# Sums of squares over a head from a rounded part and its remainder, with the rounding on ScalarE and the subtraction on GpSimd

## The reference, cut to what matters

```python
def l2norm(t):
    return t / jnp.maximum(jnp.linalg.norm(t, axis=-1, keepdims=True), 1e-12)

def attn_layer(x, Wqkv, qs, ksc, Wo):        # 16 heads of 64, window 32
    qkv = x @ Wqkv
    q, k, v = jnp.split(qkv, 3, -1)
    ...
    q = l2norm(q) * qs
    k = l2norm(k) * ksc
    ...
    q = q * cos * scale + rotate_half(q) * sin * scale
    k = k * cos * inv + rotate_half(k) * sin * inv
    out = local_attention(q, k, v)
    return out @ Wo
```

## Time and profile before

| | |
|---|---|
| median of 3 runs | 4179.59 us (4172.83 to 4183.58) |
| the profiled execution | 4182.92 us, of which the span is 4181.1 us |
| PE busy | 3900.5 us, 93% of the span |
| DVE, ACT, POOL busy | 79%, 74%, 62% |
| stage 2 | about 700 us to 4090 us, six layers |

### The profile page before, as it was taken

One profiled execution on the slowest core, in us unless ns is written; L12 is line 12 of the kernel. 1 busy time (PEld: TensorE's weight loads), 2 busy tenths in 40 slices (PEclk: granted clock), 3 DMA queues, 4 the chain that ended last, 5 costly groups with the idle time before them and its releaser, 6 DMA issues.

```text
span 4181.1 us, 190344 instructions
## 1 busy us (share of the span) xinstructions
PE 3900.5 (93%) x78816; PEld 3039.7 (73%) x78816; DVE 3305.5 (79%) x5294; ACT 3091.6 (74%) x10376; POOL 2581.2 (62%) x2583
## 2 busy tenths in 40 slices
PE   6888885999998999989999989999899999899998
PEld 3555554888866888848888668888488887588884
DVE  6778874988866888938888668989489886698894
ACT  5877785888865888838888658888488886588883
POOL 4667765766645676627666456766377664566660
PEclk9999998999999999999999999999999999999999
DMA  1000001111111111111111111111111111111110
GB/s 35 2 2 2 2 2 53 47 45 45 46 56 38 45 47 45 44 50 44 49 44 46 58 36 47 44 49 42 53 44 47 47 44 61 35 45 46 47 43 26
DMA packets 100195, 167.40 MB, mean 40 GB/s; under 512 B 26224, under 2 KB 33648, under 8 KB 99056
## 3 DMA queue, kind: packets, MB, share of 16 engines
q1 hardware_dynamic: 99312, 154.89, 12.6%
HBM read 26.13 MB, written 2.10 MB: 7 GB/s over the span
## 4 chain that ended last, share of the span: by engine, by line
PE 69%; issue 9%; POOL 3%; DVE 1%; ACT 0%; DMA 0%; SPq 0%; POOLq 0%; DVEq 0%; ACTq 0%
PE s_bank L1177 13%; PE s_bank L1246 10%; PE s_bank L1259 9%; PE s_bank L1198 8%; PE s_bank L1157 5%; PE s_proj L1222 4%; PE s_proj L1223 4%; PE s_proj L1224 4%; PE s_bank L1209 2%; PE s_bank L1210 2%; PE s_bank L1211 2%; PE s_bank L1167 2%; PE s_bank L1140 1%; POOL s_rotated L802 1%; PE s_bank L1289 1%
## 5 line engine op out<-in xcount | busy, mean ns | idle before, releaser
L802 POOL TENSOR_TENSOR s_rotated<-s_rotated,s_by_sin 128x512 f32<-128x512 f32 x768 | 983.8, 1302 | 227.3 <-DVE s_by_sin L1087 225.2
L811 POOL TENSOR_TENSOR s_probs<-s_probs,s_rden 128x256 f32<-128x256 f32 x768 | 479.7, 641 | 729.8 <-DVE s_rden L1027 729.3
L901 ACT ACTIVATE s_probs<-s_bank,s_neg_max 128x64 f32<-128x64 f32 x3072 | 908.0, 310 | 5.7 <-DVE s_neg_max L1020 5.6
L783 DVE TENSOR_TENSOR s_qk<-s_rotated,s_inv_norm 128x1024 f32<-128x1024 f32 x384 | 743.8, 1937 | 11.5
L1082 DVE TENSOR_TENSOR s_rotated<-s_proj,s_cos 128x1024 f32<-128x1024 f32 x384 | 469.6, 1223 | 241.5 <-ACT s_sq L935 240.9
L901 ACT ACTIVATION_READ_ACCUMULATOR s_probs<-s_bank,s_neg_max 128x1 f32 x3072 | 636.1, 207 | 0.0
L891 ACT ACTIVATE s_probs_t<-s_bank 64x512 f32<-64x512 f32 x384 | 226.8, 591 | 524.8 <-PE s_bank L1157 524.8
L1177 PE MATMUL s_bank<-s_qk 32*32 32x64 f32 x49152 | 581.4, 223 | 26.3 <-issue 25.9
L1177 PEld LDWEIGHTS s_bank<-s_qk 32*32 32x32 f32 x49152 | 510.9, 103 | 115.4 <-issue 114.6
L213 POOL TENSOR_TENSOR s_probs<-s_probs,s_rden 128x384 f32<-128x384 f32 (+3 forms) x512 | 406.4, 802 | 206.1 <-DVE s_rden L406 202.2
L824 POOL TENSOR_TENSOR s_sq<-s_sq 128x512 f32<-128x512 f32 x384 | 490.2, 1277 | 65.5 <-ACT s_sq L935 59.8
(11 more groups left out here) (118 smaller groups left out, 8156.2 us busy)
## 6 DMA issues: line engine op xcount, KB each, us to landing
s_v<-s_v SPq DMA_DIRECT2D x384, 192.0 KB, 2.5
s_v<-s_v SPq DMA_DIRECT2D x384, 64.0 KB, 2.4
s_qk<-f_wqk SPq DMA_DIRECT2D x6, 1024.0 KB, 6.4
s_xs_raw<-u SPq DMA_DIRECT2D x48, 128.0 KB
s_xf<-u SPq DMA_DIRECT2D x48, 128.0 KB, 2.3
s_xs_raw<-u SPq DMA_DIRECT2D x48, 127.8 KB
s_xf<-u SPq DMA_DIRECT2D x48, 127.8 KB, 2.6
s_qk<-f_wv SPq DMA_DIRECT2D x6, 512.0 KB, 6.8
```

Of the source, the lines that this page charges most:

```text
L783: return nc.vector.tensor_tensor(qk[:, quad % 2, :, :, at:at + TOKS], rotated[:, par, :, :, :], by, ALU.mult)
L802: nc.gpsimd.tensor_tensor(rotated[:, par, :, half, :], rotated[:, par, :, half, :], by_sin[:, :, 1 - half, :], (ALU.subtract, ALU.add)[half])\
L811: nc.gpsimd.tensor_tensor(part, part, by, ALU.mult).then_inc(S["probs_done"], 1)
L901: last = nc.scalar.activation(probs[:, par, h, b, :], score_bank[h][:, b * KEYS:(b + 1) * KEYS], ACT.Exp, scale=-1.0, bias=neg_max[:, par, ...
```

## The change

The sum of the halves of `sq` is split into `sum_high`, the sum rounded to float32r, and `sum_rest`, the remainder. ScalarE rounds, GpSimd subtracts, and TensorE multiplies both parts with `same_head_r` (the same ones, cast to float32r once at the start by VectorE) in one-pass products that accumulate in `ss_bank`: four float32r products of 128x256 for two float32 ones. On TensorE they now stand behind the values (L1209 to L1211 of before), on ScalarE the rounding stands ahead of L891, on GpSimd the subtraction stands between L824 and L802. `sq` is still held until `ss_done`. The core of the diff:

```diff
+        same_head_r = sb("s2_same_head_r", [P, P], F32R)
...
+        sum_high = sb("s2_sum_high", [P, 2, TOKS], F32R)
+        sum_rest = sb("s2_sum_rest", [P, 2, TOKS], F32R)
...
                     nc.gpsimd.tensor_tensor(sq[:, :, 0, :], sq[:, :, 0, :], sq[:, :, 1, :], ALU.add)\
                       .then_inc(S["sqadd_done"], 1)
+                    pool.wait_ge(S["sum_high"], m + 1)
+                    nc.gpsimd.tensor_tensor(sum_rest[:, :, :], sq[:, :, 0, :], sum_high[:, :, :].bitcast(F32), ALU.subtract)\
+                      .then_inc(S["sum_rest"], 1)
                     pool.wait_ge(S["prod_done"], 2 * m + 2)
...
+                if live(s, p, LAG_MIX, first):
+                    m = n - LAG_MIX
+                    act.wait_ge(S["sqadd_done"], m + 1)
+                    if not (first and p == LAG_MIX):
+                        act.wait_ge(S["ss_done"], m)
+                    nc.scalar.activation(sum_high[:, :, :], sq[:, :, 0, :], ACT.Copy).then_inc(S["sum_high"], 1)
...
+            nc.vector.tensor_copy(same_head_r[:, :], same_head[:, :]).then_inc(S["cast"], 1)
...
-                if live(s, p, LAG_MIX, first):
-
-                    m = n - LAG_MIX
-                    pe.wait_ge(S["sqadd_done"], m + 1)
...
-                    for i in range(2):
-                        last = nc.tensor.matmul(ss_bank[:, i * TOKS:(i + 1) * TOKS], same_head[:, :],
-                                                sq[:, i, 0, :], start=True, stop=True)
-                    last.then_inc(S["ss_done"], 1)
...
+                if live(s, p, LAG_MIX, first):
+
+                    m = n - LAG_MIX
+                    pe.wait_ge(S["sum_rest"], m + 1)
...
+                    for i in range(2):
+                        nc.tensor.matmul(ss_bank[:, i * TOKS:(i + 1) * TOKS], same_head_r[:, :],
+                                         sum_high[:, i, :], start=True, stop=False)
+                        last = nc.tensor.matmul(ss_bank[:, i * TOKS:(i + 1) * TOKS], same_head_r[:, :],
+                                                sum_rest[:, i, :], start=False, stop=True)
+                    last.then_inc(S["ss_done"], 1)
```

More of the change, by code:

```diff
@@ L659, in build_stage2 @@
         hid = [[v_flat[:, c * SEQ:(c + 1) * SEQ] for c in range((par + 1) * NC, (par + 2) * NC)] for par in range(2)]
-        names = ("const_in consts cast zeroed attn_w ffn_w tables w_high w_rest xs_in xs_high xs_rest proj_done sq_done sqadd_done prod_done "
+        names = ("const_in consts cast zeroed attn_w ffn_w tables w_high w_rest xs_in xs_high xs_rest proj_done sq_done sqadd_done sum_high sum_rest prod_done "
                  "add_done ss_done guard_done log_done inv_done norm_done score_done max_done exp_done "
@@ L986, in _ @@
             dve.wait_ge(S["consts"], 4)
-            dve.wait_ge(S["cast"], 2)
+            dve.wait_ge(S["cast"], 3)
             def centre(f):
@@ L1125, in _ @@
             pe.wait_ge(S["consts"], 4)
-            pe.wait_ge(S["cast"], 2)
+            pe.wait_ge(S["cast"], 3)
             def ffn_mean(f):
@@ L1212, in step @@
                       .then_inc(S["v_mm"], 1)
+                if live(s, p, LAG_MIX, first):
+                    m = n - LAG_MIX
+                    pe.wait_ge(S["sum_rest"], m + 1)
+                    if not (first and p == LAG_MIX):
+                        pe.wait_ge(S["guard_done"], m)
+                    if full and not first and p == LN_STEP + 1:
+                        pe.wait_ge(S["f_xc"], l * NSEQ + s)
+                    if full and not first and p == LN_STEP + 2:
+                        pe.wait_ge(S["f_log"], l * NSEQ + s)
+                    for i in range(2):
[4 more added lines that the diff above has]
+                    last.then_inc(S["ss_done"], 1)
                 if full:
```

## The result

The changed kernel takes 4414.2 us in the median (4407.49 to 4415.18), the kernel before 4176.2 over the same rounds: a ratio of 1.0564, interval 1.0544 to 1.0584. The forecast of slower came true, at 238 us where 159 were forecast; 4414 lies within the range of 4215 to 4430. The profiled execution took 4413.94 us, 231 more than that of before.

A forecast was written before the change was run, and what follows sets the result against it. TensorE bounds the kernel before at 7.36 us a step; GpSimd was to take over at 6.93 + 0.98 = 7.91 us. A layer of 507.7 against 481.2 us gives +159 us over six layers, 4339 us; range 4215 to 4430.

The forecast's parts named there:

- the bound of 4426: Upper bound of the sum: hold 1.09, copy 0.70, subtraction 1.28 us make GpSimd's round 8.14 us, adding 87 us.
- The bound moves to GpSimd, at 7.91 us a step: GpSimd's round of 6.93 us plus a 0.98 us hold sets each step, in place of TensorE's 7.36 us.
- The exclusion between `write_qk` and GpSimd: VectorE's write_qk waits for the running GpSimd instruction, then holds the next for 0.98 us, now in each step.
- The handover: Between GpSimd's addition and subtraction: 0.09 us to ScalarE, its copy 0.61, 0.09 us back.
- The place of `write_qk`: Issued 2.6 us after GpSimd's addition starts, within the subtraction; over 1.5 us of margin on either side.
- the chance of 0.75: Chance given to the main forecast, resting on the exclusion's two readings and the margin around write_qk's place.
- TensorE's saving: TensorE's own work falls 0.40 us a step, 152 us in all, coming through only if TensorE stays the bound.
- the terms for the starts of a layer and for the special steps: Per layer: -3.4 us for three steps without normalising, +9.0 for seven token splits, +3.8 for seven layer-norm holds.
- Layer norm's division, +0.54 in step 7: Layer-norm division on VectorE holds GpSimd's normalising by 0.54 us seven times a layer, +3.8 us.
- The first: Rival: TensorE stays the bound and its 0.40 us a step come through, 4028 us; chance 0.07.
- the third: Rival: GpSimd's float32r subtraction costs more, say 1.65 us, 151 us more, 4490 us; chance 0.04.
- The second: Rival: write_qk finds a free place, GpSimd is not held, a two-step chain gives 7.26 us, 4142; chance 0.13 with mixtures.

The follow-up runs named there:

- experiment 4: Kernel before plus ScalarE's rounding and GpSimd's subtraction in their new places, both unused, TensorE's sums as before: 4328.6 us, 1.035 of the kernel before.
- experiment 1: Changed kernel with write_qk's second input from an idle PSUM bank, comparison for product, normalisation left out: 4220.3 us, 1.0099 of the kernel before.
- experiments 3: Kernel before plus one unused GpSimd subtraction of 128x512 between addition and rotations, without ScalarE: 4188.7 us, 1.0024 of the kernel before.
- experiment 6: Changed kernel with all its waits and places, but the two old float32 products instead of the four one-pass ones: 4463.5 us, 1.0691 of the kernel before.

## Why the prediction was right, and what was mis-sized

The mechanism came true as it was forecast. That 4414 lies inside the range, 16 us under its upper bound, is in part luck: the bound of 4426 came from a longer round in every step (8.14 us), while the round was 7.87, below the forecast, and what brought the time up there had no term in the sum.

- **The bound moves to GpSimd, at 7.91 us a step.** Right: 7.87 in the changed kernel, and 7.86 with TensorE's side untouched (experiment 4).
- **The exclusion between `write_qk` and GpSimd, 0.98 us a step, newly on the path.** Right, and it decides: without it the kernel takes 4220 us (experiment 1). The pairs of rotations take 3.51 us at the place shown; over the whole run two rotations take 2 x 1714 = 3.43 us on average, 0.82 more than before (2 x 1302), since in 40 steps the subtraction is held in place of a rotation (its maximum is 2.27 us).
- **The handover, 0.79 us with ScalarE's copy.** Right in size (0.74 us of idle time in 294 of 384 steps; over 0.8 in the other 90, where ScalarE rounds late) and shown to be needed by experiments 3 and 4.
- **The place of `write_qk`.** Forecast 2.6 us after the addition's start, measured 1604.06 - 1601.04 = 3.02 in the step shown. The forecast had it in the subtraction in each step; it was there in 168 of 384. The margin of over 1.5 us to the wait for ScalarE, on which the chance of 0.75 rested, did not hold either: in 40 steps it fell there, nearly all of them steps 4 behind a token split or at the starts. The time hardly shows it, since a `write_qk` in the first rotation holds the second for as long.
- **TensorE's saving is hidden.** Right in plain steps. In the others it is not: up to 49 of the 152 us come through (experiment 6, the clock's part included), because there the chain over TensorE binds.
- **Mis-sized: the terms for the starts of a layer and for the special steps.** I took GpSimd's round as the only chain there, subtracted 3.4 us for the missing normalising and got 53.2 us; 58.5 were measured. Of that 1.1 us is a miscount: only two of the distances lack the normalising, and the earlier trace rows show it in the third. In these steps the chain is square, addition, rounding, subtraction, sums, projections, square, and the change puts two handovers and the subtraction into it. After the token split it runs over a long wait of TensorE. That wait costs twice where the clock falls behind it: 36 us by the 24 steps with a fall against the 12 without, and the kernel whose TensorE is kept busy there and at the starts is 66 us faster (4348 us). The slow products reach GpSimd in two ways, by a late square (0.77 us in step 4) and by a late rounding (0.73 us in step 5); the prediction priced the rounding's own time and its wait for the addition, but not the instructions ahead of it. The prediction did not look at the clock at all, although the kernel before has low steps at each layer's start and a wait of 0.9 us a step was forecast.
- **Layer norm's division, +0.54 in step 7.** Measured 8.74 - 7.86 = 0.88: the normalising is held by 0.60 us, and the rounding comes 0.26 us late, with layer-norm work ahead of it on ScalarE.
- **Rivals.** The first (TensorE stays the bound, 4028 us) and the third (a dear subtraction; its median is 1.28 us) did not happen. The second is what experiment 1 makes by force, at 4220 us in place of 4142: the price of that rival was set too low.

What stays open: how much of the last 40 us of experiment 1 above the kernel before is clock and how much other chains; why the clock falls behind 24 of 36 waits of the same length; and whether the rounding would cost less in another place on ScalarE. None of these was tried.

## What to carry to other kernels

Before giving an idle engine one more instruction, walk through its whole round, with each handover and each exclusion that it meets: here an instruction of 1.3 us cost 9 us in all (4189 us), and with 0.74 us of handover in front of it 149 (4329 us). Ask of each VectorE instruction with two SBUF inputs what GpSimd has queued behind the instruction that it waits for; a hold is free only where GpSimd would have idled anyway. Look also at what stands ahead of the new instruction on the engine that it hands over to. And where a change makes TensorE wait, look at the granted clock after the longest waits, not at the mean.

## What the runs showed of the hardware that I had not expected

- The same VectorE instruction of 128x1024 with one input in PSUM is not held at all: 1220 to 1225 ns in 360 instances, nearly all of them issued while a GpSimd instruction runs (GpSimd is busy 83% of these steps), where with both inputs in SBUF it takes 1224 to 2372.
- A wait of 2.55 us of TensorE was followed by somewhat over 3 us at 1.2 GHz, in 24 of 36 places with the same wait, and in the one shown TensorE had waited only 0.67 us in the step before and had worked without a gap for most of it. Filling part of that wait with unused products left a wait of 0.84 us and the clock at 2.4 GHz in all 36, and together with the filling at the layers' starts made a kernel of 4414 us 66 us faster.
